# Self attention of a decoder layer: value products in four 32-column tiles, row sums by GpSimd additions

## The reference

```python
def _mha(xq, xkv, w_in, b_in, w_out, b_out, bias):
    ...
    scores = jnp.einsum('bhqd,bhkd->bhqk', q, k) / jnp.sqrt(jnp.asarray(hd, xq.dtype))
    scores = scores + bias[None]
    attn = jax.nn.softmax(scores, axis=-1)
    out = jnp.einsum('bhqk,bhkd->bhqd', attn, v)
    out = out.transpose(0, 2, 1, 3).reshape(Bq, Tq, D)
    return out @ w_out.T + b_out
...
y = y + _mha(yn, yn, dec_sa_in_w, dec_sa_in_b, dec_sa_out_w, dec_sa_out_b, sb)
```

## Time and profile before

| | |
|---|---|
| median of 3 runs | 3009.94 us (3008.6 to 3010.54) |
| the profiled execution | 3011.65 us |
| its span, first to last instruction | 3009.9 us |
| PE busy | 2752.3 us, 91% |
| DVE busy | 1606.2 us, 53% |
| ACT busy | 1242.8 us, 41% |
| POOL busy | 372.6 us, 12% |
| mean granted TensorE clock | 0.956 |
| HBM read and written | 174.39 MB and 99.98 MB |

### The profile page before, as it was taken

One profiled execution on the slowest core, in us unless ns is written; L12 is line 12 of the kernel. 1 busy time (PEld: TensorE's weight loads), 2 busy tenths in 40 slices (PEclk: granted clock), 3 DMA queues, 4 the chain that ended last, 5 costly groups with the idle time before them and its releaser, 6 DMA issues. The chain is left out here.

```text
span 3009.9 us, 42480 instructions
## 1 busy us (share of the span) xinstructions
PE 2752.3 (91%) x12704; PEld 1812.9 (60%) x12704; DVE 1606.2 (53%) x3868; ACT 1242.8 (41%) x2630; POOL 372.6 (12%) x459
## 2 busy tenths in 40 slices
PE   5689987999999999999999589779969999999998
PEld 4678874444444444444444267557747777777777
DVE  4244437777777777777776266457632221222211
ACT  0032221555555555555555234278833222222222
POOL 0300002000000000000000112178546000000000
PEclk7889996999999999999999899889979999999999
DMA  9344445222222222222220577365431000000000
GB/s 287 72 163 178 171 159 136 64 65 66 65 65 65 65 65 65 65 65 65 65 65 8 124 212 223 137 175 170 139 107 37 29 28 29 1 28 28 28 14 14
DMA packets 133923, 271.62 MB, mean 90 GB/s; under 512 B 33875, under 2 KB 54867, under 8 KB 128192
## 3 DMA queue, kind: packets, MB, share of 16 engines
q1 hardware_dynamic: 128896, 254.17, 29.1%
q0 software_dynamic: 4800, 14.68, 1.7%
HBM read 174.39 MB, written 99.98 MB: 91 GB/s over the span
## 5 line engine op out<-in xcount | busy, mean ns | idle before, releaser
L970 ACT ACTIVATE sa_pr<-sa_st 128x512 f32<-128x512 f32 (+3 forms) x1280 | 611.5, 532 | 567.8 <-DVE sa_st L1033 326.3
L938 PE MATMUL sa_ov<-sa_pr,sa_v 128*33 128x512 f32 (+3 forms) x2560 | 538.6, 542 | 0.0
L1019 DVE TENSOR_REDUCE sa_part<-sa_mp 128x1 f32<-128x512 f32 (+3 forms) x768 | 411.8, 583 | 120.1 <-PE sa_mp L919 117.7
L929 PE MATMUL sa_st<-sa_q,sa_k 97*128 97x512 f32 (+3 forms) x1280 | 439.5, 413 | 24.3 <-ACT sa_pr L970 13.9
L929 PEld LDWEIGHTS sa_st<-sa_q,sa_k 97*128 97x128 f32 x1280 | 217.0, 190 | 323.4 <-ACT sa_pr L970 206.0
L919 PE MATMUL sa_mp<-sa_k,sa_q 96*128 96x512 f32 (+3 forms) x1280 | 373.8, 387 | 23.7 <-DVE sa_mp L997 19.1
L1016 DVE CUSTOM_DVE_ANT_0 sa_mp<-sa_mp,sa_ub 128x512 f32<-128x512 f32 (+3 forms) x512 | 318.0, 663 | 76.3 <-PE sa_mp L919 71.9
L1672 DVE TENSOR_TENSOR ff_hl<-ff_hf,ff_hh 128x512 fp32r<-128x512 f32 x128 | 93.5, 730 | 478.7 <-ACT ff_hh L1654 478.7
L105 PE MATMUL ff_f<-ff_ln_hi,ff_w 128*128 128x512 f32 x1024 | 343.7, 397 | 3.2 <-DVE ff_ln_lo L530 3.2
L1617 PE MATMUL ff_o<-ff_w,ff_hh 128*128 128x512 f32 x1024 | 323.9, 397 | 3.3 <-DVE ff_hl L1672 3.3
L919 PEld LDWEIGHTS sa_mp<-sa_k,sa_q 96*128 96x128 f32 x1280 | 233.5, 194 | 94.2 <-DVE sa_part L1019 23.8
(11 more groups left out here) (186 smaller groups left out, 3266.1 us busy)
## 6 DMA issues: line engine op xcount, KB each, us to landing
sa_q<-scratch_q SPq DMA_DIRECT2D x192, 128.0 KB, 4.3
sa_k<-scratch_k SPq DMA_DIRECT2D x192, 128.0 KB, 4.5
scratch_q<-qkv_qst SPq DMA_DIRECT2D x32, 512.0 KB, 3.0
scratch_k<-qkv_qst SPq DMA_DIRECT2D x32, 512.0 KB, 2.8
scratch_q<-sao_qst SPq DMA_DIRECT2D x32, 512.0 KB, 2.8
ca_q<-scratch_q SPq DMA_DIRECT2D x32, 512.0 KB, 4.3
scratch_v<-qkv_vst SPq DMA_DIRECT2D x8, 1056.0 KB, 5.2
sa_v<-scratch_v SPq DMA_DIRECT2D x16, 528.0 KB, 6.5
```

Source lines behind the costliest of these rows:

```text
L929: pe.matmul(st[bank(u, h)][:, 0:w], ks[n.par][:, h, kb * P:(kb + 1) * P], qs[n.par][:, h, g * GW + c0:(g + 1) * GW], start=True, stop=True ...
L938: last = pe.matmul(ov[64 * h:64 * h + VW, c0:GW], vs[n.par][:, kb, h, :], pr[:, u % 4, h, 0:GW - c0], start=(u in opens), stop=(u in ends))
L970: act.activation(pr[:, u % 4, h, 0:w], st[bank(u, h)][:, 0:w], ACT.Exp, scale=SCALE).then_inc(s["exp"], 1)
L1019: dve.tensor_reduce(to, tile, AX_X, ALU.max).then_inc(s["red"], 1)
```

## The change

- `values` takes two units at a time and writes four tiles of 32 columns: two heads of the even unit, two heads of the odd one. `ov` then holds two half sums for each head, all 128 rows are stored, and DRAM's `o` has 1024 rows instead of 16 x 33. The order of the units (`SELF_PAIRS`) and of the max steps is another.
- The row sums come from POOL: `add` sums a group's exponentials into `acc`, both heads at once. `SUMMED_BY_MATMUL` is empty, so no sums are made by PE besides `add_up`, which two pairs of units after a group's end multiplies `acc` with `ones` for each head (and `zeros` into the other two tiles). ACT copies `sm`, SP stores four rows.
- `pr` has 8 slots instead of 4. ACT's `exponent` waits for POOL's addition of the unit that held the slot. `mp` is three banks of one head instead of two of both, `sm` takes the bank.
- attention_out loads both halves (`ot`, `o2`); POOL's `join` adds them, ahead of the bias of two groups earlier; DVE's `multiply` waits for `joined`. The two sets of sums are added on DVE.
- Two semaphores of `SplitWeights` are kept for the whole kernel.

```diff
-SELF_ORDER = ((0, 2, 3, 1),
-              (2, 4, 1, 6, 0, 3, 7, 5),
-              (6, 10, 3, 7, 4, 11, 1, 8, 0, 9, 2, 5),
-              (5, 12, 15, 0, 1, 3, 2, 13, 8, 14, 10, 11, 7, 9, 6, 4))
+SELF_PAIRS = (((0, 1), (3, 2)),
+              ((1, 3), (5, 6), (2, 4), (7, 0)),
+              ((6, 1), (2, 9), (5, 8), (11, 10), (3, 7), (0, 4)),
+              ((0, 4), (5, 1), (14, 15), (10, 7), (6, 13), (8, 11), (9, 12), (2, 3)))
+SUMMED_BY_MATMUL = ()
+SUMS_AFTER = 2
 STEPS_FROM = 12
-STEPS_PER_UNIT = (2, 2, 1, 0, 2, 0, 1, 0, 2, 1, 1, 1, 2, 0, 2, 1, 1, 0, 2, 1,
-                  1, 2, 1, 1, 2, 1, 2, 0, 1, 1, 1, 2, 1, 0, 1, 1, 1, 2, 0, 1)
+STEPS_PER_UNIT = (3, 2, 1, 0, 2, 0, 1, 1, 1, 1, 1, 1, 1, 3, 1, 1, 1, 1, 1, 1,
...
+        pr = k.sb(f"{name}_pr", [P, NPR, 2, GW])
+        acc = [k.sb(f"{name}_acc{i}", [P, 2, GW]) for i in range(2)]
+        ssb = k.sb(f"{name}_ssb", [P, 2, GW])
+        ones = k.sb(f"{name}_ones", [P, HD])
+        zeros = k.sb(f"{name}_zeros", [P, GW])
...
             def store(n, g):
                 pair, b = place(n)
                 sp.wait_ge(s["out"], GB * n + g + 2)
-                for h in range(2):
-                    sp.dma_start(dr["o"][pair.cols(2)][h, :, b * T + g * GW:b * T + (g + 1) * GW],
-                                 osb[64 * h:64 * h + VW, g % 2, :]).then_inc(s[f"st{g % 2}"], 16)
+                sp.dma_start(dr["o"][pair.cols(P), b * T + g * GW:b * T + (g + 1) * GW], osb[:, g % 2, :])                  .then_inc(s[f"st{g % 2}"], 16)
+
+            def store_sums(n, g):
+                pair, b = place(n)
+                sp.wait_ge(s["sumout"], GB * n + g + 2)
+                sp.dma_start(dr["sum"][pair.cols(4), b * T + g * GW:b * T + (g + 1) * GW], ssb[0:P:HD, g % 2, :])\
+                  .then_inc(s[f"ss{g % 2}"], 16)
...
                 store(n, 0)
+                store_sums(n, 0)
                 row(n, 3)
                 store(n, 1)
+                store_sums(n, 1)
...
+            def add(n, u):
+                g, _, c0, _, _ = units[u]
+                i = pooled_of[g].index(u)
+                if i == 0:
+                    return
+                tile = acc[g % 2]
+                new = pr[:, u % NPR, :, 0:GW - c0]
+                pool.wait_ge(s["exp"], 2 * NU * n + 2 * u + 3)
+                if i == 1:
+                    first = pr[:, pooled_of[g][0] % NPR]
+                    waits(pool, s["summed"], GB * n + g - 1)
+                    last = pool.tensor_tensor(tile[:, :, c0:GW], first[:, :, c0:GW], new, ALU.add)
+                    if c0:
+                        last = pool.tensor_copy(tile[:, :, 0:c0], first[:, :, 0:c0])
+                    last.then_inc(s["added"], 2)
+                else:
+                    pool.wait_ge(s["added"], added(n, u) - 1)
+                    pool.tensor_tensor(tile[:, :, c0:GW], tile[:, :, c0:GW], new, ALU.add).then_inc(s["added"], 1)
+
+            def slot(n, left):
+                for u in pooled:
+                    add(n, u)
+            run(pool, N, slot, UNROLL)
...
             def values(n, u):
-                g, kb, c0, _, _ = units[u]
-                if u in opens:
+                g = units[u][0]
+                first, final = u in opens, u + 1 in ends
+                if first:
                     waits(pe, s["out"], GB * n + g + 1)
-                pe.wait_ge(s["exp"], 2 * NU * n + 2 * u + 3)
+                pe.wait_ge(s["exp"], 2 * NU * n + 2 * u + 5)
+                for i in range(2):
+                    _, kb, c0, _, _ = units[u + i]
+                    for h in range(2):
+                        tile = ov[HD * (2 * i + h):HD * (2 * i + h + 1)]
+                        v = vs[n.par][:, kb, h, 0:HD]
+                        if first and c0:
+                            pe.matmul(tile[:, 0:c0], v, zeros[:, 0:c0], start=True, stop=True)
+                        last = pe.matmul(tile[:, c0:GW], v, pr[:, (u + i) % NPR, h, 0:GW - c0], start=first, stop=final)
+                if u in direct:
+                    if u == direct_of[g][0]:
+                        pe.wait_ge(s["sumout"], GB * n + g + 1)
+                    for i in range(2):
+                        c0 = units[u + i][2]
+                        for h in range(2):
+                            last = pe.matmul(sm[HD * (2 * i + h):HD * (2 * i + h + 1), c0:GW], ones[:],
+                                             pr[:, (u + i) % NPR, h, 0:GW - c0], start=(u == direct_of[g][0]),
+                                             stop=(i == 1 and u == direct_of[g][-2]))
+                last.then_inc(s["av"], 2)
+
+            def add_up(n, g):
+                pe.wait_ge(s["added"], added(n, pooled_of[g][-1]))
+                if not direct_of[g]:
+                    pe.wait_ge(s["sumout"], GB * n + g + 1)
+                    for h in range(2):
+                        pe.matmul(sm[HD * (2 + h):HD * (3 + h)], ones[:], zeros[:], start=True, stop=True)
                 for h in range(2):
-                    last = pe.matmul(ov[64 * h:64 * h + VW, c0:GW], vs[n.par][:, kb, h, :],
-                                     pr[:, u % 4, h, 0:GW - c0], start=(u in opens), stop=(u in ends))
-                last.then_inc(s["av"], 1)
+                    last = pe.matmul(sm[HD * h:HD * (h + 1)], ones[:], acc[g % 2][:, h, :], start=not direct_of[g], stop=True)
+                last.then_inc(s["summed"], 1)
...
             def exponent(n, u):
                 w = GW - units[u][2]
-                waits(act, s["av"], NU * n + u - 2)
+                waits(act, s["av"], NU * n + u - NPR + 2)
+                v = (u - NPR) % NU
+                if v in pooled:
+                    waits(act, s["added"], added(n, v) - (NA if u < NPR else 0))
...
+            def empty_sums(n, g):
+                act.wait_ge(s["summed"], GB * n + g + 1)
+                waits(act, s[f"ss{g % 2}"], (16 * GB // 2) * n + 16 * (g // 2))
+                act.activation(ssb[:, g % 2, :], sm[:], ACT.Copy).then_inc(s["sumout"], 1)
...
+                for x, t in enumerate((ot, o2)):
+                    for j in range(2):
+                        sp.dma_start(t[2 * HD * j:2 * HD * (j + 1), g.par],
+                                     dr["o"].rearrange("(c j x r) t -> x j r c t", j=2, x=2, r=2 * HD)[x, j, :, :, g.cols(GW)])\
+                          .then_inc(s[f"o{g.par}"], 16)
...
+            def join(g):
+                pool.wait_ge(s[f"o{g.par}"], 64 * g.uses + 64)
+                for c in range(KC):
+                    pool.tensor_tensor(ot[:, g.par, c, :], ot[:, g.par, c, :], o2[:, g.par, c, :], ALU.add)\
+                        .then_inc(s["joined"], 1)
+
+            join(Step(0, 0))
+            join(Step(0, 1))
             pool.wait_ge(s["cols"], ncol)
 
             def slot(g, left):
+                if left >= 2:
+                    join(g + 2)
                 pool.wait_ge(s[f"y{g.par}"], 16 * g.uses + 16)
                 for i in range(TT):
                     pool.tensor_tensor(y[:, g.par, i, :], y[:, g.par, i, :], brow[:], ALU.add).then_inc(s["biased"], 1)
-            run(pool, NG, slot)
+            run(pool, NG, slot, tail=2)
...
             def multiply(g, c):
                 if c == 0:
-                    dve.wait_ge(s[f"o{g.par}"], 128 * g.uses + 128)
+                    dve.wait_ge(s[f"r{g.par}"], 64 * g.uses + 64)
+                dve.wait_ge(s["joined"], KC * g + c + 1)
                 dve.tensor_tensor(ot[:, g.par, c, :], ot[:, g.par, c, :], rb[:, g.par, c, :], ALU.mult)\
```

More of the change, by code:

```diff
@@ L723, in self_units @@
     out = []
-    for g, order in enumerate(SELF_ORDER):
+    for g, pairs in enumerate(SELF_PAIRS):
+        order = [kb for pair in pairs for kb in pair]
         assert sorted(order) == list(range(TT * (g + 1))) and order[0] <= TT * g
@@ L800, in emptied, with reduced, added, sums_due @@
         return max(i for i in range(2 * NU) if i % NST == j) - 2 * NU
+    def reduced(a, h):
+        j = 2 * a + h
+        if j >= NMP:
+            return j - NMP
+        return max(i for i in range(2 * NM) if i % NMP == j) - 2 * NM
+    def added(n, u):
+        return NA * n + pooled.index(u) + 1
+    def sums_due(n, u):
+        if u + 1 in sums_at:
+            yield n, sums_at[u + 1]
+        if u + 1 + NU in sums_at and not (isinstance(n.n, int) and n.n == 0):
+            yield n + -1, sums_at[u + 1 + NU]
+    def sums_left():
+        last = Step(N // UNROLL - 1, UNROLL - 1, UNROLL)
+        return [(last, sums_at[u]) for u in sorted(sums_at) if u >= NU]
     def after(n, u, left):
@@ L1686, in transformer @@
     y1, y2 = scratch("y1", (P, NG * TT, D)), scratch("y2", (P, NG * TT, D))
-    o = scratch("o", (H, VW, TOK))
+    o, sums = scratch("o", (2 * D, TOK)), scratch("sum", (2 * H, TOK))
     dr = {
```

114 lines of the change are left out of this document (71 added, 43 removed).

## The result

The changed kernel takes 3174.2 us (median of 4 runs, 3170.9 to 3175.5) against 3009.3 us of the kernel before (3004.1 to 3010.5) on the same chip: ratio 1.055, 95% interval 1.053 to 1.057. It is slower by 165 us; forecast were 3127 us and a range of 3050 to 3195. The profiled execution took 3170.87 us (span 3169.0).

The account below looks back on a forecast made before the run. TensorE was taken to pace self attention before the change and GpSimd after it; in attention_out, TensorE and VectorE were nearly closed loops. Self attention +33 and attention_out +84 made +117 us on the median, 3127 us, range 3050 to 3195.

Parts of the forecast that it names:

- +33 forecast: Self attention: GpSimd becomes the pace at 75.3 us a step; +31, with the last products, copy and store +33 us.
- The gap of 0.09 us an addition: Self attention on GpSimd: gap between dependent additions, times 36 is 3.2 us a step.
- rival A: Self attention: GpSimd dearer, 80 us a step or more, giving 3202 us; chance 0.17.
- PE then needs about 61 us: Self attention: TensorE's need a step after the change, 74.1 - 16.9 + 3.4 us.
- the tiling: Self attention's value products: four column tiles at a time instead of two take 16.9 us a step off TensorE.
- the products for the sums: Self attention: four products with ones per group add 0.85 us a group on TensorE, 3.4 a step.
- rivals C and D: Self attention: C, cheaper GpSimd, 70 us a step, 3047, chance 0.15; D, value products pay, 64 us, 2957, chance 0.06.
- PE busy for less than 90%: Self attention: expected sign, TensorE under 90% busy in the windows while GpSimd is above 90%.
- +84 forecast: attention_out: ramp +19, next group +9, and 14 us for each of four groups, together +84 us.
- Groups 2 to 5: attention_out: 14 us each, from the residual addition 10.6 later, 2.0 for contention and 1.5 for clock.
- the second megabyte: attention_out: doubled value loads land in 7.7 us instead of 5.7, at some 350 GB/s, partly beside the issue.
- Ramp: Start of attention_out: bias of group 0 waits behind a join, 8.4 MB at 255 GB/s; +19, next group +9.

Follow-up runs that it names:

- narrow additions: Changed kernel, with GpSimd's additions from the third unit of a group on covering only 64 columns, so most row sums are left out: 3100.4 us.
- bias first: Changed kernel, with GpSimd's four bias additions of group g in attention_out ahead of the join of group g+2: 3095.3 us.
- tiny join: Kernel with the bias ahead of the join, all loads kept, each join addition made on 16 of 512 columns: 3068.0 us.
- the best run: Changed kernel with both edits: six additions a step moved from GpSimd to TensorE, and the bias ahead of the join: 3050.5 us.

## Why the prediction was right, and where its sizes were off

**Self attention, +33 forecast, +40.7 measured.** GpSimd does set the pace, at the forecast price: 75.8 us a step against 75.3, and 15 times 0.5 is the missing 8. The gap of 0.09 us an addition was right (0.08 in the median), and waits for ScalarE (25 us in all) make up the small rest. VectorE's instructions weren't stretched (the maxima over 512 columns of L1016, now L1140, take 0.71 us in the mean before and after), as the earlier trace rows said. That rival A's 80 us didn't come was said by the line of the earlier trace rows.

**The failed step is beside the sum:** "PE then needs about 61 us." Without GpSimd's load the step is 72.6 us, 68.3 of them TensorE's. Three terms were wrong.

The first is the tiling. The earlier trace rows was misread: it isn't two full units. Its eight records by form (1670.05 to 1671.70), and two full units of the kernel before:

```profile
L938 PE MATMUL sa_ov<-sa_pr,sa_v 128*33 128x512 f32 x4 | 1.1, 605 | 0.0
L938 PE MATMUL sa_ov<-sa_pr,sa_v 128*33 128x384 f32 x4 | 0.8, 486 | 0.0
```

```profile
1002.83 1.91 PE L938 MATMUL sa_ov<-sa_pr,sa_v 128*33 128x512 f32 x8
```

Two full units go from 1.91 us to 1.07 at full clock. Over a step the tiling saves 12 us instead of 16.9, in part because eight of the twenty pairs hold units of unequal width, and in four tiles a pair takes the time of its wider unit. The second is the products for the sums, 1.08 us a group where 0.85 was taken, 4.4 a step. The third stood at nothing: the products for the maxima, whose scratch `mp` shrank from four banks to three. TensorE's lines in the ten steps of the kernel before, then in the run with narrow additions (its windows hold 13.5 and 13.8 steps):

```profile
L938 PE MATMUL sa_ov<-sa_pr,sa_v 128*33 128x512 f32 (+3 forms) x2152 | 449.7, 539 | 0.0
...
L919 PE MATMUL sa_mp<-sa_k,sa_q 96*128 96x512 f32 (+3 forms) x1078 | 304.9, 376 | 1.4 <-DVE sa_part L1016 0.2
```

```profile
L1002 PE MATMUL sa_mp<-sa_k,sa_q 96*128 96x512 f32 (+3 forms) x1099 | 367.3, 402 | 30.5 <-DVE sa_part L1140 14.2 <-DVE sa_part L1143 8.3 <-DVE sa_neg L1129 4.1
L1028 PE MATMUL sa_ov<-sa_pr,sa_v 128*32 128x512 f32 (+3 forms) x2200 | 287.4, 568 | 0.0
```

A step's maxima products are busy for 26.7 us instead of 22.6, and TensorE stands idle ahead of them for 2.2 us instead of 0.1, mostly for VectorE's reductions: 6 us, half of what the tiling saves. The lower clock (0.96 against 0.99) is in these numbers. That the missing bank is the cause is not shown, since the order of the units changed too and no run gives the bank back. The old tiling in the new form costs 10.8 us a step more than before: 3.1 are waits, 3.8 more busy time of the maxima products, and the products for the sums explain the 4 or so that remain. So rivals C and D weren't open at all: a step of 64 or 70 us lies under TensorE's 72.6, whatever GpSimd's price. It was luck that this did no harm to the forecast: it counted on 14 us between GpSimd's pace and TensorE's, and there were 3. One of its own signs, PE busy for less than 90%, failed for this reason (92%).

**attention_out, +84 forecast, +119.8 measured.** The mechanism was the one laid out, and each wait is where it was said, but the sum lies outside the +55 to +110 of the forecast; the total stays in its range because self attention was near. Its terms, from the residual additions:

- Groups 2 to 5: 4 times 18.4 instead of 14. The first residual stands 16 us later in the period instead of 10.6, since the doubled loads take 14.7 us from issue to join, not 9.4. I had charged the second megabyte 2 us net (at some 350 GB/s, half of it hidden); it costs 5.5. The rest of the period costs some 2.5 (3.5 taken for contention and clock together).
- Ramp: +32.5 instead of +19 for group 0, +11.0 instead of 9 for group 1. The bytes ahead of `join(2)` passed at 223 GB/s (1747.7 to 1788.0), not 255, and the store of the inverse took 7.4 us behind the loads, not 3.2.
- Groups 6 and 7: +3 where I had none.

By cause, the 119.8 are 78.9 for the order (bias first), 28.2 for the join beside VectorE once the order is mended (tiny join), and 12.7 for the rest, mostly the ramp's longer loads. The first two overlap: in the changed kernel the joins ran while VectorE stood idle, so the collision cost little there. What it costs where they meet: a bias that met VectorE took 5.4 us instead of 5.0 for its four in the changed kernel, and in the run with the bias first a join cost the normalisation 2.3 to 3.5 us in five of the eight groups (the 3.8 of an expectation above is four times the longest). The "SBUF — State Buffer" page of the Trainium skill (Who interferes with whom) says of GpSimd and a VectorE instruction in a 2-port mode that whoever issues first keeps the shared ports for its whole instruction and the other is blocked. The trace agrees in kind only: beside each other a normalisation took 1.48 us and a join 1.44, one for one, which is more than either alone (0.54 and 1.25) and less than the two together (1.8); in which mode the normalisation ran, no run shows. Which of the two costs counts is decided by what stands beside what, and the order decides that.

**The bound for a better version.** Six additions on TensorE bring self attention to 3.6 to 11.6 us above the kernel before (three profiles of it), and attention_out with joins of 16 columns still is 12.7 above: of the pieces with the full output none is under the kernel before, and the best run is 3050.5 us. Self attention with nearly no additions is 36 us under it (1652.3 against 1688.3), so cheap row sums are where a gain would have to come from; no run has them.

## What to carry to other kernels

Work moved off a full engine is worth the distance to the next limit: sum up what the new form adds to the full engine itself, and take GpSimd's price per element (2.4 ns at 1024, gap included) before giving it all the additions. On an in-order queue, put what is wanted next ahead of what must wait for a load; here two swapped blocks were worth 79 us. When a load is doubled and something waits for it, charge its bytes at the rate of the window in which it is waited for (218 to 223 GB/s here, at DMA shares of 0.92 to 0.99), not at a higher one. When a kernel gives up a scratch bank, charge the producer's waits for it.
